# Contextual attention in two layers: loops over units written out, four pieces of work reordered

## The reference, cut to what matters

```python
raw_w, _, _ = extract_patches(b, 4, 2)            # 1600 patches of 64 x 4 x 4
f = b[:, :, ::2, ::2]                             # 40 x 40
w, Hs, Ws = extract_patches(f, 3, 1)              # 1600 patches of 64 x 3 x 3
wn = w / max(norm(w), 1e-4)
yi = einsum('bpd,bld->blp', w, wn)                # scores, 1600 x 1600
yi = softmax(yi * mm * 10.0, axis=1) * mm
patches = einsum('blp,bld->bpd', yi, raw_w)
out = overlapping 4x4 patches added up at stride 2, cropped by one pixel, / 4
```

## Time and profile before

| what | value |
| --- | --- |
| median of three runs | 1543.32 us |
| profiled execution, its own time | 1549.3 us |
| its span, first to last instruction | 1547.5 us |
| PE busy | 1389.9 us (90%) |
| DVE busy | 1226.9 us (79%) |
| ACT busy | 860.8 us (56%) |
| chain that ended last | PE 40%, DVE 18%, issue 13%, SPq 12%, ACT 8%, DMA 6% |
| mean granted clock of TensorE | 0.971 |

### The profile page before, as it was taken

How to read it: one execution, slowest core, us unless ns; L and a number is a source line. 1 busy time by engine, 2 the same in 40 slices (tenths; PEclk the granted TensorE clock), 3 DMA queues, 4 the chain that set the end, 5 groups by cost and what they waited for, 6 DMA issues and landing times.

```text
span 1547.5 us, 28187 instructions
## 1 busy us (share of the span) xinstructions
PE 1389.9 (90%) x7190; PEld 906.0 (59%) x7190; DVE 1226.9 (79%) x2831; ACT 860.8 (56%) x2233; POOL 54.6 (4%) x63
## 2 busy tenths in 40 slices
PE   4978999889998899988999889997999889999896
PEld 4755655656557565565656566565665656556333
DVE  4668888778888788887898777977779788887983
ACT  2676555646557465583555644656545655557431
POOL 1001000010000100001000000001000010000100
PEclk9998999999999999999999999998999999999998
DMA  5305352273522653145631545315462153522442
GB/s 97 44 1 152 96 119 73 61 161 86 114 66 78 153 105 104 50 108 134 122 87 45 130 113 116 86 51 138 106 120 76 50 148 92 120 66 81 124 137 60
DMA packets 181676, 149.67 MB, mean 97 GB/s; under 512 B 119986, under 2 KB 177394, under 8 KB 181490
## 3 DMA queue, kind: packets, MB, share of 16 engines
q1 hardware_dynamic: 181170, 146.60, 39.8%
q10 hardware_dynamic: 320, 0.99, 0.3%
HBM read 19.76 MB, written 13.11 MB: 21 GB/s over the span
## 4 chain that ended last, share of the span: by engine, by line
PE 40%; DVE 18%; issue 13%; SPq 12%; ACT 8%; DMA 6%; DVEq 1%; ACTq 1%; POOL 0%; POOLq 0%
PE psO L511 18%; PE psG L461 17%; SPq L307 5%; DVE G L921 4%; DVE G L861 4%; DVE S L867 3%; DMA SH<-G 3%; PE psG L470 3%; DVE Z L954 3%; ACT S L680 3%; DVE G L932 3%; SPq L255 3%; SPq L295 2%; DMA HV<-LOHI 2%; ACT G L666 2%
## 5 line engine op out<-in xcount | busy, mean ns | idle before, releaser
L511 PE MATMUL psO<-Z,B 123*128 123x492 f32 (+1 forms) x1792 | 768.0, 557 | 41.8 <-ACT OSB L700 22.6
L511 PEld LDWEIGHTS psO<-Z,B 123*128 123x128 f32 x1792 | 327.5, 195 | 266.7 <-issue 179.5
L461 PE MATMUL psG<-LH,HL 128*123 128x246 f16 (+2 forms) x2616 | 411.0, 287 | 26.2 <-issue 19.7
L461 PEld LDWEIGHTS psG<-LH,HL 128*123 128x123 f16 x2616 | 280.5, 138 | 166.2 <-issue 112.5
L867 DVE CUSTOM_DVE_ANT_0 S<-G,RB 123x492 f32<-123x492 f32 (+1 forms) x448 | 268.9, 606 | 94.4 <-DVE G L861 53.9
L691 ACT ACTIVATE G<-G,nb 123x492 f32<-123x492 f32 (+1 forms) x448 | 270.2, 649 | 106.7 <-DVE G L921 105.9
L680 ACT ACTIVATE S<-S,nm 123x480 f32<-123x480 f32 (+3 forms) x560 | 306.7, 553 | 4.2 <-DVE nm L872 4.1
L921 DVE SCALAR_TENSOR_TENSOR G<-G,RA,psB 123x492 f32<-123x492 f32 (+1 forms) x448 | 275.2, 657 | 20.5 <-issue 19.6
L932 DVE TENSOR_TENSOR G<-G,SH 123x492 f32<-123x492 f32 (+1 forms) x448 | 251.4, 600 | 42.9 <-DMA SH<-G 42.5
L666 ACT ACTIVATE G<-psG 123x492 f32<-123x492 f32 (+3 forms) x256 | 120.3, 473 | 216.1 <-PE psG L461 127.4
L653 ACT ACTIVATE G<-psG 123x246 f32<-123x246 f32 (+1 forms) x136 | 64.4, 474 | 262.5 <-PE psG L461 262.2
(11 more groups left out here) (84 smaller groups left out, 585.7 us busy)
## 6 DMA issues: line engine op xcount, KB each, us to landing
SH<-G SPq DMA_DIRECT2D x336, 214.8 KB
SH<-G SPq DMA_DIRECT2D x112, 107.2 KB
SH<-G SPq DMA_DIRECT2D x336, 19.2 KB
XP<-x SPq DMA_DIRECT2D x20, 280.0 KB, 6.0
XP<-mid SPq DMA_DIRECT2D x20, 280.0 KB, 5.3
mid<-OSB SPq DMA_DIRECT2D x52, 80.0 KB, 2.3
out<-OSB SPq DMA_DIRECT2D x52, 80.0 KB, 2.3
HL<-LOHI SPq DMA_DIRECT2D x16, 246.5 KB, 3.5
```

The costliest lines, as they stand in the source:

```text
L461: last = pe.matmul(psG[0:TW, bank, b0 * TW:b1 * TW], st[:, p:p + TW], mv[:, lo:lo + n], start=i == 0, stop=i == len(terms) - 1)
L511: last = pe.matmul(psO[:, b, 0:n], B[:, o:o + 128], Z[:, 2 * (s % 2) + j, 0:n], start=t == 0, stop=t == TILES - 1)
```

## The change

All loops over units become Python loops, so every unit's instructions stand in the program once, with constant addresses and constant values to wait for. Four pieces of work get another place:

- PE, first step of a chunk (7, 14, 21): `odd_tile` comes before the first paste instead of behind it.
- PE: `lse_row(.., 1)` moves from the end of a body into step 2 of the next body, behind the first paste and ahead of the odd tile.
- ACT: `score_sums` of the pair before, in steps 6, 13, 20 and 27, moves behind the `read_out` of the next step.
- ACT: the last `block_group` (of step 27) moves to the end of step 28. PE's call for it moves from the end of step 27 to the start of step 28, with nothing between the two places.

```diff
-            def one(tensor, b):
-                if isinstance(b, int):
-                    return tensor[b]
-                return tensor[bass.ds(b, 1)].rearrange("o c h w -> (o c) h w")
+            def source(u):
+                return None if u is None else (x, mid)[u // IMAGES][u % IMAGES]
...
-            body(None, 0, 1, one(x, 1), one(x, 0), None)
-            with sp.Fori(0, 2) as b:
-                body(b, b + 1, b + 2, one(x, b + 2), one(x, b + 1), one(mid, b))
-            body(2, 3, 4, one(mid, 0), one(x, 3), one(mid, 2))
-            body(3, 4, 5, one(mid, 1), one(mid, 0), one(mid, 3))
-            with sp.Fori(0, 2) as b:
-                body(b + 4, b + 5, b + 6, one(mid, b + 2), one(mid, b + 1), one(out, b))
-            body(6, 7, None, None, one(mid, 3), one(out, 2))
-            body(7, None, None, None, None, one(out, 3))
+            body(None, 0, 1, source(1), source(0), None)
+            for u in range(UNITS):
+                v, w = (n if n < UNITS else None for n in (u + 1, u + 2))
+                body(u, v, w, source(w), source(v), (mid, out)[u // IMAGES][u % IMAGES])
...
PE body:
+                    first = at is not None and at[2] == 0
+                    if s == SLOTS and v is not None:
+                        block_group(v, w, PAIRS - 1)
                     if pairs:
                         even_tile(v, pairs[0])
+                    if pairs and first:
+                        odd_tile(v, pairs[0])
                     if at:
                         paste_tile(at, s, 0)
-                    if pairs:
+                    if s == FIRST and u is not None:
+                        lse_row(u, v, 1)
+                    if pairs and not first:
                         odd_tile(v, pairs[0])
...
-                    if v is not None and 21 <= s <= SLOTS - 1:
+                    if v is not None and 21 <= s < SLOTS - 1:
                         block_group(v, w, s - 21)
...
-                if v is not None:
-                    lse_row(v, w, 1)
...
ACT body:
+                    if s % PAIRS == 0 and v is not None:
+                        score_sums(v, score_list(s - 1)[0] - 1)
...
-                        if j:
+                        if j and (s + 1) % PAIRS:
                             score_sums(v, j - 1)
...
-                    if v is not None and (NK - 1) * PAIRS <= s < SLOTS:
-                        g = s - (NK - 1) * PAIRS
-                        block_group(u, v, g)
+                    if v is not None and (NK - 1) * PAIRS <= s < SLOTS - 1:
+                        block_group(u, v, s - (NK - 1) * PAIRS)
+                    if v is not None and s == SLOTS:
+                        block_group(u, v, PAIRS - 1)
...
PE, ACT, DVE (POOL likewise with UNITS - 1):
-            with pe.Fori(0, UNITS - 2) as u:
+            for u in range(UNITS - 2):
                 body(u, u + 1, u + 2)
```

More of the change, by code:

```diff
@@ L778, in _ @@
             body(None, 0, 1)
-            with act.Fori(0, UNITS - 2) as u:
+            for u in range(UNITS - 2):
                 body(u, u + 1, u + 2)
@@ L1037, in _ @@
             body(None, 0, 1)
-            with dve.Fori(0, UNITS - 2) as u:
+            for u in range(UNITS - 2):
                 body(u, u + 1, u + 2)
@@ L1070, in _ @@
             body(None, 0)
-            with pool.Fori(0, UNITS - 1) as u:
+            for u in range(UNITS - 1):
                 body(u, u + 1)
```

## The result

The changed kernel takes 1500.65 us, median of four runs (1498.19 to 1502.71), beside 1543.88 us for the kernel before on the same chip: ratio 0.971, 95% interval 0.9677 to 0.9742, 43 us faster. I had forecast 1519 us with 1503 to 1533 as range: the direction was right, the size 18 us too small. The profiled execution took 1502.71 us.

What follows compares the result with a forecast made beforehand. PE was held by instruction waits at five loop turns (19.7 us) and read-out waits (22.6 us), elsewhere by DVE. Terms -19.5 - 2.8 - 5.2 + 3.0 = -24.5 us gave 1524.8, scaled to 1519 us; range 1503 to 1533.

Steps and rivals of the forecast that it cites:

- the zero for register work on PE, ACT and DVE: Wait values and addresses no longer computed in unit bodies: nothing gained, since step 11 to 16 takes equal time written out.
- the zero for the clock: TensorE's half speed after the pause at a turn: pause ahead of step 2 stays, so no change.
- the size of step 7: PE's read-out wait goes, but DVE limits the gain to 0.86 us in six units: 5.2 us, bounds 0 and 11.3.
- gaps at the jumps: Five loop turns, PE idle ahead of the first score products: 3.9 us each, 19.5 us gained, bounds 17 and 21.
- SP written out: register work and two jumps: SP's queue between steps 8 and 11: register work 0.70 us in four bodies, 2.8 us gained, bounds 0 and 3.9.
- `lse_row` in step 2: Four transposes lose their free place before the layout copy: 0.43 us in 7 bodies, 3.0 us lost, bounds 0 and 4.8.
- steps 7, 14, 21, 28: Reorderings there: 5.2 us gained, all in step 7; steps 14, 21 and 28 nothing.
- The lock by DVE: PE stands in step 16 some 37.6 us after DVE got SH in step 11, so only an earlier SH helps.
- rival 4: At the turn, no pause long enough for the clock to fall: 11.9 us more gained, 1507 us; chance 0.09.
- The rival from the 108 ns: At the turns: the gap is not the jump's and stays; sum -5.5 us, 1538 us; chance 0.04.
- rival 1: In written-out bodies: instruction starvation, stalls of 3.9 us; with two in each 1566 us, slower; chance 0.04.

Runs made afterwards that it cites:

- experiment 2: Kernel before with only a hint to each sequencer, at the top of each iteration, of where the loop's jump goes; 1526.18 us beside 1548.51, ratio 0.9865.
- experiment 6: Old order, all loops written out, with only the move of lse_row into step 2: 1514.28 us, ratio 0.9781; changed kernel with that move undone: 1495.42 us, 0.9659.
- experiment 1: Kernel before with only the loops written out, old order of work: 1509.71 us, ratio 0.9745 to the kernel before.
- experiment 9: Changed kernel plus 24 idle transposes on PE in the pause ahead of the layout copies: 1499.73 us, ratio 0.9686 to the kernel before.
- the second run of experiment 1: Kernel before with only the four reorderings, all loops kept: 1545.18 us beside 1547.81, ratio 0.9984.

## Why the forecast missed

By the ratios, times 1545 us, the 45 us divide as below. The medians give the same picture within a few microseconds, and each step is good to 4 or 5 us. The steps of the prediction that failed are the zero for register work on PE, ACT and DVE, the zero for the clock, and the size of step 7.

| step | forecast | measured | from the ratios |
| --- | --- | --- | --- |
| hint on all loops: gaps at the jumps, and the clock behind them | -19.5, clock 0 | -20.9 | 0.9865 to 1 |
| PE, ACT, DVE, POOL written out: register work | 0 | -10.4 | 0.9798 to 0.9865 |
| SP written out: register work and two jumps | -2.8 | -6.8 | 0.9754 to 0.9798 |
| `lse_row` in step 2 | +3.0 | +4.2 | 0.9781 to 0.9754 |
| steps 7, 14, 21, 28 | -5.2 | -11.0 | 0.971 to 0.9781 |

**Loops: right, and a little more than the gap.** The five turns went, as did their "issue" group. That they were a wait for instructions, not the jump's own time, is shown by experiment 2. The distance between starts fell by 5.5 us at a turn in that trace: 3.5 of it the gap, 1.4 the clock behind it. In the time some of this is missing.

**Register work: this step failed.** "On DVE, ACT and PE I put this at nothing" rested on one stretch, step 11 to step 16, that takes the same time in and out of the loop. The next stretch, step 16 to `lse_row` in step 24, differs in the trace of before by 0.7 us, most of it PE's wait for `lse` (2.65 us against 2.07), and I didn't look at it. That is 4.3 us. The other 6 of the 10.4 are not pinned to a place: in the pair of traces the looped bodies differ by 4.9 us in all, and the larger part of what the spans differ by lies outside them, where PE, ACT and DVE have no register work in either kernel. So 4 to 5 us of register work are shown; whether the rest is more than the spread of these runs is open. What the hint itself costs, one more instruction at the top of each iteration, is in the 10.4 us too.

**Step 7: right mechanism, wrong size.** PE's wait went, the exponentials then waited for DVE, as I had said, but the gain is 11.0 us (with the other reorderings, of which step 28 is nothing), not 5.2, at the upper end of my bounds, 11.3. I had taken all but 0.86 of PE's 1.9 us to come back as a wait in step 11, and the clock as untouched by it. At full clock the exponentials of step 8 come 1.1 us earlier (39.4 us after the start against 40.5 in experiment 6), and the wait in step 11 is 0 to 0.67 us. The lock by DVE that I had read from the earlier trace rows is looser in the changed kernel and in experiment 1: from `SH` to step 16 the bodies of units 0 to 5 take 37.7 to 39.2 us, not always 37.7. And in the written-out kernel without these edits the pause cost half-speed clock in three of six bodies; that is up to 5 of the 6 us missing, but as the number of such bodies varies from run to run, luck has a part in this size. The kernel before shows 1.00 in this place in all six bodies, so I could not have read this fall from it. A further 0.2 us per body comes in step 21, between step 16 and step 24: 50.75 us against 50.97, and 50.97 again with the paste first. I had put it at 0.

**Clock: wrong at zero, and rival 4 came half true.** Over 8 us behind the seven starts PE loses 13.6 us to the clock in the trace of before, 6.6 in that of the changed kernel, where it is 1.00 behind three starts and 0.79 to 0.81 behind four. These 7 us are part of what the table puts on the jumps, less what the move of `lse_row` costs again. The rest, which rival 4 also counted in its 11.9, is 6.5 us in the traces and 1 to 4 us in the time (experiment 9).

**SP and lse_row: right in sign**, too small by 4 us and by 1.2, both within what the runs can tell apart. SP's stretch of step 8 to 11, which I had put at 23 us in all units, is 21.3 to 23.0. The 0.43 us of `lse_row` were right, the clock behind a longer wait was left out.

**Range.** Its low end added the best cases of the terms that I had priced, and rival 4. Two causes priced at nothing, register work and the clock in step 7, lay outside it.

The rival from the 108 ns of the Trainium skill (Advanced Engine Details and Errata, section Control Flow Timing) falls as a price for these turns: they cost 3.9 us each without the hint. With it a turn left nothing beyond a wait of 0.28 to 0.5 us for the copy, so for the jump alone no run contradicts the figure. The same skill's Runtime: NRT & Kernel Launch, section Instruction fetch mechanics, that a taken jump outside the loaded pages stalls, agrees with experiment 2. Starvation of straight code (rival 1) was not seen in any run: in the changed kernel PE's "issue" waits inside bodies are at most 0.5 us long, and the seven of 1.9 us in experiment 1 stand in step 28, where the kernel before waits as long for the read-out.

## What to carry to other kernels

If a hardware loop's body is long, look for PE's idle time "issue" at its first instruction: a prefetch hint for the jump back took 21 of 43 us here without writing anything out. To tell whether register work costs something, compare every stretch of a looped body with its written-out copy, not one, and look first where an engine waits for a chain of short steps on others. A pause that is taken from TensorE can be worth more than its length, 1.7 us here where the granted clock behind it was 0.79 over 8 us, and whether the clock falls can be seen only in the kernel that has the other changes.

## Not expected of the hardware

A wait of 1.9 us in step 7 left the granted clock at 1.00 in all six bodies of the kernel before, and at 0.79 over 8 us in three of six once the loops were written out, although the wait is as long. What the bodies did before it differs: over the seven traces with the old step 7, 20 of the 42 bodies had a fall behind their start, and 2 of these fell again in step 7; of the 22 that began at full clock 9 did. The kernel before belongs to the first kind in all six. This is a count, no run tests it alone.

And the two last bodies together, from the start of unit 6's to the end, took 281.6 to 283.9 us in the three kernels whose PE comes out of a hardware loop (before, the second run of experiment 1, and experiment 2), and 276.0 to 280.7 in the twelve others; why is open.
